# The head loop of TensorE starts at a multiple of 256 instructions

## What is computed

```
def step(Sm, inp):
    q_, k_, v_, g_, b_ = inp
    Sm = Sm * jnp.exp(g_)[..., None, None]
    kv = jnp.einsum('bhk,bhkv->bhv', k_, Sm)
    delta = (v_ - kv) * b_[..., None]
    Sm = Sm + jnp.einsum('bhk,bhv->bhkv', k_, delta)
    o = jnp.einsum('bhk,bhkv->bhv', q_, Sm)
    return (Sm, o)
```

## Time and profile before

| | us |
|---|---|
| runs of the kernel | 3558.36, 3521.67, 3533.22 |
| median | 3533.22 |
| the profiled execution's own time | 3533.24 |
| its span, first to last instruction | 3531.3 |
| loop, from PE's first loop branch to its last (15 passes) | 2569.0 |

### The profile page before, as it was taken

One profiled execution on the slowest core, in us unless ns is written; L12 is line 12 of the kernel. 1 busy time (PEld: TensorE's weight loads), 2 busy tenths in 40 slices (PEclk: granted clock), 3 DMA queues, 4 the chain that ended last, 5 costly groups with the idle time before them and its releaser, 6 DMA issues. The chain is left out here.

```text
span 3531.3 us, 130838 instructions
## 1 busy us (share of the span) xinstructions
PE 2847.5 (81%) x52455; PEld 2353.6 (67%) x52456; DVE 2466.0 (70%) x5044; ACT 1759.1 (50%) x5564; POOL 1162.6 (33%) x1093
## 2 busy tenths in 40 slices
PE   1004989898989898989989898989898989837778
PEld 1003878787878787877777787878777877624445
DVE  5804777777767777767776777776777777547776
ACT  1002566665656566556665665656565666401111
POOL 0574332333323233323232323232323333243320
PEclk8556999999989899999999999999999999868888
DMA  3101111111010101010111111111111111041110
GB/s 125 59 25 44 31 36 30 39 33 44 22 44 22 44 23 44 22 44 24 44 36 30 36 30 36 33 33 39 31 37 32 34 36 30 5 135 54 54 42 12
DMA packets 84571, 138.94 MB, mean 39 GB/s; under 512 B 16378, under 2 KB 54453, under 8 KB 83523
## 3 DMA queue, kind: packets, MB, share of 16 engines
q1 hardware_dynamic: 62435, 97.57, 9.3%
q0 software_dynamic: 12288, 24.19, 2.2%
q10 hardware_dynamic: 9216, 8.39, 0.7%
HBM read 103.58 MB, written 35.91 MB: 40 GB/s over the span
## 5 line engine op out<-in xcount | busy, mean ns | idle before, releaser
L1091 DVE SCALAR_TENSOR_TENSOR p_y<-p_xr,p_cw,p_y 128x512 f32<-128x512 f32 x768 | 670.9, 880 | 128.5 <-ACT p_y L875 109.2
L616 PE MATMUL p_psF<-xnS,p_w_hl 128*128 128x512 f32 x1536 | 440.0, 431 | 193.8 <-PEq L531 131.6
L616 PEld LDWEIGHTS p_psF<-xnS,p_w_hl 128*128 128x128 f32 x1536 | 297.4, 204 | 260.7 <-POOL p_w_hl L498 131.9
L933 ACT ACTIVATE p_Xs<-p_psI 128x256 f32<-128x256 f32 (+1 forms) x386 | 161.7, 419 | 621.0 <-PE p_psI L660 457.6
L1293 POOL TENSOR_TENSOR p_E<-p_E,p_sj 128x512 f32<-128x512 f32 x128 | 130.7, 1042 | 943.4 <-DVE p_sj L1116 943.4
L1134 DVE TENSOR_TENSOR p_ATP<-p_psF,p_E 128x512 f32<-128x512 f32 x256 | 165.6, 687 | 240.2 <-PE p_psF L647 227.8
L1301 POOL TENSOR_TENSOR p_M<-p_ATc,p_masks 128x512 f32<-128x512 f32 x128 | 169.7, 1331 | 403.5 <-ACT p_ATc L913 383.7
L660 PEld LDWEIGHTS p_psI<-p_Dc,p_M 32*32 32x32 f32 x16384 | 174.6, 107 | 144.8 <-issue 136.2
L660 PE MATMUL p_psI<-p_Dc,p_M 32*32 32x32 f32 x16384 | 206.3, 196 | 74.7 <-DVE p_DTc L1152 56.9
L781 PE MATMUL p_psO<-p_wout,p_ont 128*128 128x256 f32 x1056 | 247.8, 389 | 0.9 <-ACT p_ont L964 0.7
L669 PEld LDWEIGHTS p_psI<-p_Xs,p_DTc 32*32 32x32 f32 x16384 | 173.1, 107 | 108.2 <-issue 100.2
(11 more groups left out here) (296 smaller groups left out, 6605.2 us busy)
## 6 DMA issues: line engine op xcount, KB each, us to landing
p_ab<-decays SPq DMA_DIRECT2D x64, 512.0 KB, 5.3
p_w_raw<-in_w_in SPq DMA_DIRECT2D x17, 768.0 KB, 4.0
p_wgu<-in_w_gu SPq DMA_DIRECT2D x64, 176.0 KB
expert_in<-p_zero SPq DMA_DIRECT2D x16, 512.0 KB, 6.8
p_xe<-expert_in SPq DMA_DIRECT2D x64, 128.0 KB
expert_out<-p_ye ACTq DMA_DIRECT2D x64, 128.0 KB, 1.9
p_wd<-in_w_down SPq DMA_DIRECT2D x64, 88.0 KB
p_wout<-in_w_out SPq DMA_DIRECT2D x16, 256.0 KB, 3.3
```

Of the source, the lines that this page charges most:

```text
L616: m = pe.matmul(b4(psF[f % 2][:, :]), w_hl[:, wp, kt, ty * P:(ty + 1) * P], xnS[:, xp, kt, :].rearrange("p (b t) -> p b t", b=B)[:, :, c * ...
L933: act.activation(dst, src, ACT.Copy).then_inc(s["xs" if l < 5 else "join_xs"], 1)
L1091: m = dve.scalar_tensor_tensor(y[:, ty, :, :], xr[:, ty, :, tap:tap + P], cw[:, ty, tap:tap + 1], y[:, ty, :, :], ALU.mult, ALU.add)
```

## The change

```diff
     start, end, marks = name + "_loop", name + "_end", []
     regs = nc.alloc_registers(name + "_i", engines=[engine])
     nc.regs_mov(regs, 0)
+    if engine == mybir.EngineType.PE:
+        nc.engines[engine].addr_align(256, offset=0, max_nops=0)
     nc.br(start, engines=[engine])
     with nc.body(start, valid_engines=[engine]):
```

## The result

The changed kernel took 3612.12 us (median of 4 runs, 3606.18 to 3616.97), the kernel before 3533.22 (4 runs, 3521.67 to 3558.36). The ratio is 1.0213, 95% interval 1.0155 to 1.027. Forecast were 3489 us and a range of 3440 to 3530.

The account below looks back on a forecast made before the run. PE was taken to set the pace, idling 8.1 us of each pass on late instructions. 15 passes x 3.4 us x 0.87 = 44 us off 3533.24 gave 3489 us, range 3440 to 3530.

Parts of the forecast that it names:

- What bounds the kernel: PE sets the pace; its largest idle item is late instructions at 256-instruction block crossings, 8.1 us of each pass.
- A and B: Loop branch's target block fetched earlier, and the crossing at 6600 removed: together worth 3.4 us of a pass.
- the case that the wait holds the request back: Wait ahead of `level_y` (position 6486) delays the target block's request by 0.9 us; gain then 2.5 us of a pass.
- Nothing else takes the place of this idle time at once: Behind the branch ACT idles 5.63 us and DVE 4.88, so both start earlier by what PE gains.
- The share of 0.87: Part of PE's time that reaches the end: 8.9 us more of PE made a pass 7.7 us longer.
- C: Other block crossings move 56 instructions later: taken as nothing, with ends of -1 and +2 us of a pass.
- The sign named for a wrong forecast: The forecast is wrong if the stops of step 0 sum to over 3 us.
- the other one: The forecast is wrong if the passes shrink by less than the idle time that PE loses.
- R4: Rival, chance 0.08: step 0 becomes bound by its blocks, 4.9 us each; with the branch gain failing, 3599 us.
- E: PE's clock behind the branch: taken as 0, with 2.2 us of a pass kept as an end.
- R2: Rival, chance 0.11: DVE, in a chain with PE in the levels, absorbs the gain; only 0.3 passes, 3518 us.

Follow-up runs that it names:

- e1: Changed kernel with the loop head at slot 56 of a block instead of slot 0: 3541.78 us, ratio 1.0004 to the kernel before.
- e2: Changed kernel (slot 0) with the expert's three loads in step 0 issued ahead of the 768 KB weight load: 3472.75 us, ratio 0.9806.
- e3: Kernel before (slot 56) with the expert's three loads in step 0 issued ahead of the 768 KB weight load: 3513.17 us, ratio 0.9924.
- e6: Changed kernel (slot 0) without PE's branch prefetch hint: 3599.13 us, ratio 1.0154.
- e7: e4 without PE's branch prefetch hint: 3449.84 us, ratio 0.9730.
- e4: Changed kernel with the loop head at slot 39 and the expert's loads ahead of the 768 KB load: 3406.73 us, ratio 0.9640.
- e5: Changed kernel with the loop head at slot 39 instead of slot 0, SP's load order unchanged: 3578.73 us, ratio 1.0093.
- e10: e5 with 16 extra matmuls on PE before its wait for the expert's load, head at slot 7 to keep later crossings: 3527.50 us, ratio 0.9974.
- e8: e4 with the loop head at slot 152 instead of slot 39: 3477.47 us, ratio 0.9829.

## Why the prediction was wrong, point by point

- **What bounds the kernel.** That the stops are block crossings, that the head stood at slot 56, and where the new crossings would be: right (e1, the positions 768, 1024 and 1280 as counted, 427 packets). That "issue" is the largest idle item: right.
- **A and B, 3.4 us at the first L616**: right in size. Measured 3.18, and the branch at 1.60 us, where 1.35 to 2.3 was named for the case that the wait holds the request back.
- **"Nothing else takes the place of this idle time at once"**: this is the step that failed. ACT and DVE were looked at, PE's own next wait was not. Its row (20.9 us in 15 passes, for the expert's load) was in the answer from which the earlier trace rows were copied. It said that the load was already the last thing to come: PE stood ready for it 1.4 us of each pass too early. What PE won ahead of it could reach the end only by the 0.4 us that the load itself moved: of 3.2 us won, 0.4 were left at L791, and behind `project_out` PE was 1.2 us late. e2, e3, e6 and e7 show it from both sides: the hint's gain at the branch is worth 43 us with the load out of the way (e4 against e7) and nothing clear of the noise with it (after against e6).
- **The share of 0.87** compared passes in which all of PE's work was stretched. It is no price for an advance at one point, which stops at the next late arrival.
- **C, taken as nothing with +2 us as its end**: the second step that failed, mis-sized. The stops of all other crossings were 3.3 us of a pass before, as counted, and are 6.8 after, +3.5 instead of nothing. For step 0, 2.2 us were given by the two stops of step 2; its stops are 2.8 us, and its levels take 3.7 us longer, since the fall of the clock in it was left out. (The sign named for a wrong forecast, over 3 us of stops in step 0, was just not met; the other one, passes that shrink by less than PE's idle time, was.) Against that the loss of step 2's own stops was set. But step 2 kept stops, 3.0 us in all at 4352, 4608 and 4864 against 2.1 before: 4608 and 4864 lie in the `level_y` of levels 3 and 4, and the prediction set only 0.7 us for steps 1 to 3 beside 0.4 at 4352, where the traces have 4.1 in all. e2 against e4 confirms the size: 4.7 us of a pass between slots 0 and 39 with all else equal. The blocks of step 0 had passed in 3.7 us each, and that was known; the nearer reading of it was that all of them are close to the limit, not that two are. A later packet, as told in the last section, makes a block take up to 5.2 us, which R4 took (4.9) and C did not.
- **E, the clock, taken as nothing**: half right. The first 12 L618 did get the full clock (3.20 us for 5.11 in the mean), and `project_out` lost it (5.39 for 3.92), where the idle time had moved and grown. e5 and e10, alike but for the filling work, differ by 51 us.
- **The rivals.** R4 named the right side (3599) with a chance of 0.08, and its place, step 0, is where two thirds of the loss are. That its number is near is luck: its other half, that the branch would not get faster, is false, and the late load, which it does not name, did that part's work; its 4.7 us of stops in step 0 were 2.7. R2 had the gain absorbed, but by DVE. A rival that names PE's next wait was missing.

What stays open: why the lower clock of e5 reaches steps whose idle time did not grow. That it does is in the traces. From 1655 to 3294, e5 and e10 have the same idle time (2.4 and 2.2 us of a pass), but 8.0 and 4.8 us at the lower clock, and e5 takes 1.7 us longer there; the two differ in code only at the head. And the changed kernel's loss at slot 0 is not a plain sum: slot 0 against 39 costs 33 us with the load behind, 66 with the loads first, 64 with PE kept busy (by the ratios 1.2, 1.7 and 1.9%).

## What to carry to other kernels

Before an idle stretch is counted as won, read the same engine's next wait: the transfer or engine named there, and how much it has to spare, is the bound of the gain, and an earlier arrival can cost more than it wins if the longer idle stretch lowers TensorE's clock. In a loop whose body is fetched anew in each pass (here 427 blocks for 16 passes of 26 and the rest), the place of its head is a parameter worth some 2% (3407 to 3477 us here by the slot alone); the stops' counts in the timeline tell the present slot, and the slot to try is one at which the branch is late in its block and dense runs of small instructions are not cut. Order the small loads that are needed first ahead of a large one that is gated by a late event.

## What the runs showed of the hardware that was not expected

- A branch hint on PE works when the branch's block has been entered early enough: 1.40 to 1.63 us with 216 to 255 instructions between entry and branch, 2.91 with 112 (e8), 3.38 to 3.50 us with 16, 3.60 to 3.74 without a hint at 215 and 254.
- Where PE stops at a crossing, 3.3 to 5.3 us in the mean have passed since it started the instruction at the crossing ahead (before: 3.6 from 6344 to 6600, 5.1 from 4040 to 4296). What hardly changes is the last part: PE goes on 2.2 to 3.0 us (in the middle 2.4 to 2.5) after a packet of its instruction queue starts, in 426 stops over 0.3 us of six traces. What changes is when the packet starts, 1.1 us after the crossing at 6344 (before) and 1.2 after 512 (after), but 2.5 to 2.7 after those at 4040 and 4296 (before), 768 and 1024 (after). Why it starts later there no run isolates. Nor must a stop follow: 3784 to 4040 (before) passes in 3.06 us and 1384 to 1640 (e8) in 2.19 without one.
- By the Trainium skill ("Runtime: NRT & Kernel Launch", Instruction fetch mechanics) the cost of crossing a block of 256 instructions is mostly hidden. By their count that holds here: about 5 of the 26 crossings of a pass before show a stop. But those 5 cost 4.6 us of a pass, and the place of the head alone moves the kernel by 2% (e4 and e8), so for dense runs of small products the measurement decides: they cannot be left out.
- Behind a wait of 6.0 us in the mean (after), `project_out` ran at full speed in none of 15 passes, behind 1.4 us (before) in 12. The wait quoted above had a granted 0.77 and the 5.3 us behind it 0.67, between the two levels of 1.2 and 2.4 GHz.
